# Moving GpSimd's three checks on TensorE's progress one group of gathers ahead in a graph-attention kernel

## What is computed

```python
def gnn(x, edge_index, W, att_src, att_dst, bias):      # 4 heads of 64
    h = (x @ W).reshape(-1, H, DOUT)
    a_src = einsum('nhd,hd->nh', h, att_src); a_dst = einsum('nhd,hd->nh', h, att_dst)
    e = leaky_relu(a_src[src] + a_dst[dst], 0.2)
    ex = exp(e - segment_max(e, dst)[dst])
    alpha = ex / segment_sum(ex, dst)[dst]
    return sigmoid(segment_sum(alpha[:, :, None] * h[src], dst) + bias)
def mix(x): ...      # q, softmax over keys, context, gate from a small GELU layer, projection
def ffn(x): ...      # top-k rows of a routing weight go through w1 (256x1024), GELU, w2 (1024x256)
xn = layernorm(x)
x = x + gnn(xn, ...) + mix(xn)
return x + ffn(layernorm(x))
```

## Time and profile before

| | us |
|---|---|
| median of 3 runs | 1705.45 |
| lowest, highest | 1705.07, 1711.49 |
| the profiled execution, and its span | 1712.47, 1710.7 |
| mean granted TensorE clock in it, as a share of 2.4 GHz | 0.808 |

### The profile page before, as it was taken

How to read it: one execution, slowest core, us unless ns; L and a number is a source line. 1 busy time by engine, 2 the same in 40 slices (tenths; PEclk the granted TensorE clock), 3 DMA queues, 4 the chain that set the end, 5 groups by cost and what they waited for, 6 DMA issues and landing times. The chain is left out here.

```text
span 1710.7 us, 24314 instructions
## 1 busy us (share of the span) xinstructions
PE 1160.9 (68%) x5815; PEld 839.4 (49%) x5815; DVE 1043.3 (61%) x2649; ACT 532.2 (31%) x1154; POOL 855.2 (50%) x891
## 2 busy tenths in 40 slices
PE   5985545555567777676876677666777666677772
PEld 4653333333345554454554455454555544555662
DVE  6663245455666666656766666666676666676657
ACT  4442222231223323323333333333232332332530
POOL 0603235443666565565655665656665656665000
PEclk8997667786668887888877887888888888888887
DMA  9244254443555455445544454554454445454104
GB/s 257 73 102 114 56 150 131 115 121 85 137 145 131 131 138 131 123 129 131 135 124 128 128 142 125 131 133 132 127 142 126 128 131 139 127 138 129 44 0 150
DMA packets 165874, 212.03 MB, mean 124 GB/s; under 512 B 49492, under 2 KB 131220, under 8 KB 165672
## 3 DMA queue, kind: packets, MB, share of 16 engines
q0 software_dynamic: 39984, 110.94, 25.9%
q1 hardware_dynamic: 117538, 97.15, 19.7%
q10 hardware_dynamic: 8306, 3.41, 0.9%
HBM read 165.93 MB, written 45.46 MB: 124 GB/s over the span
## 5 line engine op out<-in xcount | busy, mean ns | idle before, releaser
L755 POOL DMA_INDIRECT ring<-feat_d,idx x832 | 817.0, 982 | 627.4 <-issue 433.0
L1730 PE MATMUL bank<-ring,hot 128*64 128x265 f32 x1664 | 271.9, 472 | 153.6 <-issue 89.7
L1730 PEld LDWEIGHTS bank<-ring,hot 128*64 128x64 f32 x1664 | 150.1, 167 | 266.6 <-issue 186.4
L1310 DVE TENSOR_TENSOR ring<-ring,bank 128x1024 f32<-128x1024 f32 x208 | 239.8, 1215 | 1.8 <-ACT bank L1503 1.4
L1765 PE MATMUL bank<-late,w_s 128*128 128x256 f32 x768 | 229.9, 460 | 0.4 <-ACT hT L1552 0.4
L1765 PEld LDWEIGHTS bank<-late,w_s 128*128 128x128 f32 x768 | 182.4, 241 | 36.3 <-ACT hT L1552 0.5
L1702 PE MATMUL bank<-w_s,hT 128*128 128x256 f32 x784 | 198.2, 410 | 1.9 <-ACT hT L1552 1.9
L1702 PEld LDWEIGHTS bank<-w_s,hT 128*128 128x128 f32 x784 | 158.3, 207 | 27.6 <-ACT hT L1552 2.8
L1681 PE MATMUL bank<-ident,lk 128*16 128x128 f32 x208 | 43.8, 351 | 187.7 <-issue 115.3
L1503 ACT ACTIVATE bank<-diff 128x64 f32<-128x64 f32 x52 | 11.8, 228 | 434.7 <-DVE diff L1294 289.4
L1552 ACT ACTIVATE hT<-bank,b_s 128x256 f32<-128x256 f32 x192 | 77.3, 473 | 141.8 <-remote 130.6
(11 more groups left out here) (271 smaller groups left out, 1756.3 us busy)
## 6 DMA issues: line engine op xcount, KB each, us to landing
parts_d<-zero SPq DMA_DIRECT2D x59, 265.0 KB
parts_d<-wout SPq DMA_DIRECT2D x208, 66.2 KB
lists<-dloc_d SPq DMA_DIRECT2D x104, 128.0 KB
ring<-feat_d,idx POOLq DMA_INDIRECT x832
parts<-parts_d SPq DMA_DIRECT2D x49, 265.0 KB
xs<-in_x SPq DMA_DIRECT2D x50, 128.0 KB
big<-in_x SPq DMA_DIRECT2D x7, 896.0 KB, 11.0
out<-xnT SPq DMA_DIRECT2D x7, 896.0 KB, 4.2
```

The lines of the kernel that those rows point to most:

```text
L755: pool.indirect_dma_start(out=ring[:, u * TI + q, 0:AW], out_offset=None, in_=feat_d, in_offset=bass.IndirectOffsetOnAxis(ap=idx[:, u, q:q ...
L1310: V.tensor_tensor(feats, feats, ex[:, g * TG:(g + 1) * TG, :].unsqueeze(3) .to_broadcast([P, TG, HEADS, HD]), ALU.mult).then_inc(S("scaled ...
L1730: mm = T.matmul(bank[2 + n][c * WIN:(c + 1) * WIN, 0:SW], hot[:, q, :], ring[:, u * TI + q, 0:SW], start=(j == 0), stop=(j == TG - 1))
```

## The change

Of the three pace checks, those on `turn_scores` and `turn_maxima` stand at group 1 and 2 instead of 2 and 3; group 0 gets a new check, that TensorE has made the target scores of tile k-1 (`scores_done`, made by `scores_ahead` in body k-2, right behind the sums); group 3 and the second layer have none any more.

```diff
@@ fill(k, u) on GpSimd @@
-                        if g == 1 and not known_below(k, LAG_OUT + 1):
-                            pace = ("ff2_done", number(pool, k - LAG_OUT))
-                        if g >= 2 and not known_below(k, 1):
-                            pace = (("scores_turned", "max_turned")[g - 2], number(pool, k))
+                        if g == 0 and not known_below(k, 1):
+                            pace = ("scores_done", number(pool, k))
+                        if g in (1, 2) and not known_below(k, 1):
+                            pace = (("scores_turned", "max_turned")[g - 1], number(pool, k))
```

## The result

The changed kernel took 1778.89 us (median of 4 runs, 1773.32 to 1781.36) beside 1705.26 us for the kernel before (4 runs, 1694.30 to 1711.49): a ratio of 1.043, 95% interval 1.038 to 1.048. It is slower by 74 us. The forecast was 1689 us, with a range of 1648 to 1745.

The account below looks back on a forecast made before the run. TensorE's finished work told late behind long gather runs was taken as the bound; 39 bodies x 0.4 = 16 us gained, other parts nothing, so 1705.45 - 16 = 1689 us, range 1648 to 1745.

Parts of the forecast that it names:

- What bounds the kernel: Main loop: TensorE's finished work is told late in a long run of gathers, coming through about 2 us after it.
- Groups 0 to 2: Moved checks: holds of the gates and of the turned maxima should go, the maxima falling 4 us into a run.
- Worth up to 99 us: Turned maxima on VectorE: removing their holds saves 99 us in the loop, the upper end of the gain.
- Group 3, the run of twelve: Groups 1 to 3 become one run of twelve gathers; mean body 25.6 us, 0.4 less than now, 16 us gained.
- Odd bodies: Loop bodies with the second layer behind the sums: half taken as held, 24.2 us each.
- the slower rival: The run of twelve holds the sums in odd bodies too: about 27 us for all, 1744 us; chance 0.33.
- Held bodies: Bodies whose sums are held by the run of twelve, all even ones included: 16.3 + 10.6 = 26.9 us.
- The outer bound: If all loop bodies are held at the longest tail, 27.4 us each, 55 us are lost.
- Start of the program: Bodies 0 to 10: put at nothing; tile 1's later start of first groups hidden by the rows' slack.
- No change, "the amount and not its shape": Rival for the loop: the amount of gathering counts, so gains at the maxima are lost at the sums; 1705 us; chance 0.22.
- Rows too late: Rival: gathered rows landing in 4 us, not 1.5, cost under 10 us in all; no chance of its own.
- The signs that I had named: Profile after: gathers four, pause, twelve, pause; L1290 under 20 us, L1552 above 101.8, L1533 falling; odd bodies 24, even 27.

Follow-up runs that it names:

- e10: The changed kernel with one more check: group 3 waits for the first half of the previous tile's sums; 1689.2 us beside 1712.8, ratio 0.985.
- after_again: The changed kernel run again unchanged in another job; 1397.1 us beside 1391.5 for the kernel before, ratio 1.004.
- e2_no_scores: The changed kernel without its new check on the target scores at group 0; 1396.7 us beside 1390.8 for the kernel before, ratio 1.005.
- before_again: The kernel before run again unchanged in another job, for a trace; 1391.5 us.
- e6_narrow: The changed kernel with gathers of half the bytes from the third tile on; 1397.3 us beside 1391.2 for the kernel before, ratio 1.005.

## Why the prediction was wrong

**What bounds the kernel.** The reading of the late job's profile held: TensorE's words come about 2 us behind a long run of gathers and pass early in it. The trace after repeats it in both kinds of body, and e10 moves the end of the run by four gathers and the word with it. The pattern is looser than the section put it: a word can also be told within the run, as the first activations of body 24. In body 26 of the kernel before too, 27 of the 32 sums had run at full pace; only the last five stalled. What the section could not tell, and took as given, is that the gathers are the reason by themselves. In prompt jobs an unbroken run of 576 gathers holds nothing.

**Groups 0 to 2.** Right in their mechanism. The maxima pass, 1.5 us at most, as said for a signal 4 us into a run, and the wait for them is gone. The gates' "remote" wait is gone too. "Worth up to 99 us" was the upper bound, and none of it reached the time.

**Group 3, the run of twelve: the step that failed.** The prediction took even bodies as held, 26.9 us, and *half* of the odd ones, 24.2 us, "since the sums' signals are due earlier in the run". TensorE's turns give 28.4 us in even bodies (mean of 18) and 27.3 in odd ones (mean of 18). Two terms were mis-sized:

- Odd bodies, 3.1 us each; 2.7 of it is the step from "half held" (24.2) to held (26.9). The sums do come earlier, and in body 25 TensorE runs them at full pace (2.01 us for 16 records). But in all 18 odd bodies ScalarE keeps them only 2.2 to 2.6 us behind the run, so none is free of the hold, and the root, `normed` and the next scores follow from there. The prediction took "due earlier" for "in time"; it also left out what stands behind the sums on TensorE in an odd body, which ends last in 6 of the 18. This is the mechanism of the slower rival, which was given 0.33.
- Held bodies, 1.5 us each in the even ones. In body 24 the run starts 1.55 us behind the turn, not 0.9, and the turn comes 11.25 us behind the run's end, not 10.6. Over the 18 even bodies the tail is 11.0 to 12.3 us, 11.6 on average. In the kernel before the same tail had 9.8 to 11.5 us; I used its middle. One part of the longer tail can be seen: seven sums of body 24 are still to come when the run ends, where body 26 of the kernel before had three, and ScalarE waits another 0.97 us for them before it keeps the second half.

The mean is 27.8 instead of 25.6 us. 39 bodies x 2.2 = 86 us. The profiled execution missed its forecast by 81 us (1777.1 against 1696.5), the median by 90 (1778.9 against 1689). The outer bound was mis-added as well: a longest tail of 9.8 + 1.7 = 11.5 us gives 16.3 + 11.5 = 27.8 us a body and 70 us lost, some 1775, where the prediction wrote 27.4 and 55. Its own rows thus held the measured body at their edge. The slower rival had the right sign and half the size (1744): it took 27 us for all bodies, and 1.0 instead of 1.8 us more per body.

**Start of the program.** Priced at nothing. In the late job tiles 0 to 7 were 10.2 us faster and tiles 7 to 13 11.1 us slower, which cancel. In prompt jobs the start is where the whole effect lies, 7.2 us up to tile 7 in after_again. The 7.4 us stop at tile 1's group 0 is part of it, so "hidden by the rows' slack as well" was wrong there. It isn't all: e2_no_scores, without that check, stops 5.3 us at tile 1's group 1 and is still 4.0 us behind at tile 7.

**No change, "the amount and not its shape".** In late jobs it is out: same 16 gathers per tile, 26.0, 27.8 and 26.1 us a body with three placements of the pauses. The rule that I had set beside it, of the Trainium skill's page "SBUF — State Buffer", section "SBUF: two separate sides" (engine ports and DMA ports are disjoint, neither slows the other), agrees with the prompt jobs' traces, 3.80 us for the sums amid gathers. In the late job's traces the sums' single records, which start 0.7 to 1.7 us apart in body 24, stand against it, as far as timing can say.

**Rows too late.** No wait of VectorE for rows at L1261 appears in the waits after, as said.

**The signs that I had named.** Four, pause, twelve, pause: seen in all 36 tiles. L1290 under 20 us "remote": no row. L1552 above 101.8: 225.0. L1533 falls: its "remote" row is gone. "Odd bodies come to 24, even ones to 27": 27.3 and 28.4. The condition for being wrong on the high side, L1345 waiting over 5 us in odd and even bodies alike, is nearly met: 269.4 us in 32 instructions, 8.4 each.

## What to carry to other kernels

A pause for pacing doesn't remove a wait; it picks which signal falls into the next uninterrupted stretch. Before moving one, write down for each kind of body every signal that is due in each stretch, and what is queued behind it, not only the one that looks late today. And a kernel tuned by such pauses is tuned to a condition: here three placements lie up to 6% apart in the two late jobs and 1% apart in prompt ones, in which no pause at all does as well as the kernel before. Run the unchanged kernel again in another job before believing a gain or a loss of this size.

## What the runs showed of the hardware

- The same program took 1391 to 1394 us in nine jobs and 1705 to 1713 in two, on one chip in both ways, and within each job all of the runs compared here keep to one of the two. The two traces of the kernel before run alike up to the first gather (at 154.8 and 156.3 us; TensorE busy 116.8 and 116.3 us, granted clock 0.91 and 0.90). From then on TensorE's words are late in one and not in the other, though a gather takes 980 and 982 ns. The cause isn't settled: not the code, not the chip alone, not the length of a gather. Other work on the machine and where the program's memory lies weren't tried and can't be told from these traces.
- TensorE's mean granted clock was 0.86 in prompt jobs and 0.79 to 0.82 in late ones. From tile 13 to 49 TensorE was busy 17.0 us a body in before_again, 18.5 in the kernel before and 20.0 in the changed one, at a granted clock of 0.88, 0.83 and 0.79, so 1.5 of the 5.5 us between the first two could be longer matmuls; the rest stands in waits. A word can be late at full clock: the granted clock was 1.00 while VectorE waited for the maxima of body 20 (790.7 to 796.2 us of the kernel before) and from 908.2 to 920.95 us in the changed kernel, where ScalarE's first activations of body 24 waited. So a low clock at that moment isn't what holds them. What lowers the mean clock of a whole job stays open.
- The words seen late are TensorE's. In the late trace of the kernel before, TensorE's turn of the scores starts 0.05 to 0.14 us behind VectorE's last score (L1270) in all 36 bodies from 13 to 48, 31 of them within a run of gathers, up to 8.0 us into it. No such turn falls later in a run, so later is not shown.
- A gather of 128 rows takes GpSimd 0.98 us with a gap of 0.30 us, whether it moves 260 columns or 130 (982 ns on average in the kernel before, 976 in e6_narrow).
- Version to keep: in a late job e10 took 1689 us where the changed kernel had taken 1779 in another; against the kernel before (0.985 [0.969, 1.000], two runs against three) it isn't clear of noise. In a prompt job it is the slowest of all (1.011). None of the kernels run is shown to beat the kernel before in either kind of job.
